# Full attention in a six-stage transformer kernel: four heads in four row strips, scores made twice, no transposed probabilities

## Chip, cores, metric

One NeuronCore of a Trainium2 chip runs the kernel alone. The metric is the device time of one execution in microseconds (us); less is better. Everything is float32 unless said otherwise.

## What is computed

Activations are 2048 tokens (4 sequences of 512) of 128 features. The reference runs six blocks on them: an expert layer, a linear attention, the expert layer again, a local-window transformer of 6 layers, a full softmax attention, and the local transformer again; each block is fed a layer norm of x and added to x. The change touches only the full attention, cut here to what matters:

```python
# 16 heads of 8 features, B=4 sequences, T=512 tokens
q, k, v, kp = heads(x @ W_Q.T), heads(x @ W_K.T), heads(x @ W_V.T), heads(x @ W_K_prime.T)
attn   = softmax(q @ k.T  / sqrt(8))      # [b, h, 512, 512]
attn_p = softmax(q @ kp.T / sqrt(8))
out = alpha * (attn @ v) + (1 - alpha) * (attn_p @ v)
x = x + merge(out) @ W_O.T
```

There are two score tables per head: one with k, one with kp. That makes 4 x 16 x 2 tables of 512x512.

## The kernel before

The kernel is one program with its instructions written out engine by engine; the engines meet at semaphores, and each engine works through its own list in the order of the code. x and its normed copy xh lie in SBUF as [feature, token] for the whole run. Between two stages all engines meet at a barrier, so a stage's time is its own. The stages are called at the end of `program`: `layernorm_block`, `expert_block` and so on; the full attention is `full_attention_block`, between the layer norms ln4 and ln5.

That stage loops over the four sequences (a hardware loop, `Fori`, on each engine). For a sequence it prepares first: TensorE projects 128 tokens at a time on `w4` (L1223, q, k, k' and v side by side). ScalarE and VectorE then split q, k and k' into three bf16 parts each (`part`, `rest`: L1294, L1297, L1362, L1365), VectorE and GpSimd lay the nine products of parts side by side in `stack` (72 rows a head, L1368, L1334), TensorE turns `stack` (L1238), and ScalarE and VectorE copy the result to `QK` (L1300, L1375). So one bf16 matmul of 72 rows makes f32-like scores.

Then come 64 units, one for each head and each 128 queries. A unit passes round the engines:

- TensorE makes both tables' scores for 128 queries x 512 keys in two PSUM banks (L1256, bf16).
- VectorE takes the negative row maximum of both banks in one operation (L1386).
- ScalarE does exp(score - maximum), with the row sum beside it (L1307, two of them, each followed by a read of the sum).
- VectorE makes the weights alpha / sum and (1 - alpha) / sum (L1391, L1393); GpSimd multiplies the first table by its weight (L1341); VectorE multiplies the second and adds (L1381, three units later).
- TensorE turns the mixed probabilities in four 128x128 blocks (L1264, four units later), and ScalarE copies them to `PT` (L1314).
- TensorE multiplies them with V (L1274, five units later) into a 32-row strip of bank 6. After 16 units ScalarE copies that bank (L1320), and TensorE multiplies with `wo_full` (L1248). At the end of a sequence VectorE adds the result to x (L1395).

The two score bank pairs (banks 0 and 1, 2 and 3) alternate from unit to unit, and so do the two turn banks (4 and 5). The steps MIX, TURN and PV (3, 4, 5 units) set how far the later steps run behind.

In the profile "psum" is any PSUM bank, and "full_x" the tile x of this stage. An f32 matmul leaves two records in the trace, a bf16 matmul and a transpose one.

Of the kernel before, what the change touches and what calls it, by code (L numbers as in the profile page):

```python
# [13 lines left out]
P = 128  # L14
# [1158 lines left out]
def full_attention_block(nc, M, W):  # L1173


    GROUP = 4 * TILES
    UNITS = AH * TILES
    MIX, TURN, PV = 3, 4, 5
    with ExitStack() as ctx:
        sem = stage_semaphores(nc, ctx, "full")  # L1180
        sb = lambda n, s, d=F32: ctx.enter_context(nc.sbuf_tensor(f"full_{n}", s, d))
        proj_full, part_ready, rest_ready, v_ready, q_stacked, k_stacked = (
            sem(n) for n in ("proj_full", "part_ready", "rest_ready", "v_ready", "q_stacked", "k_stacked"))
        stack_full, stack_act, stack_dve, prepared = (
            sem(n) for n in ("stack_full", "stack_act", "stack_dve", "prepared"))
        score_full, max_ready, exp_done, recip_ready, coef_ready, weighted, mixed = (
            sem(n) for n in ("score_full", "max_ready", "exp_done", "recip_ready", "coef_ready", "weighted", "mixed"))
        pt_full, pt_ready, out_full, out_ready, y_full, x_updated, cleared = (
            sem(n) for n in ("pt_full", "pt_ready", "out_full", "out_ready", "y_full", "x_updated", "cleared"))
        coefs = sb("coefs", [P, 2])  # L1190
        part = sb("part", [P, 2, SPLITS, 3 * D], BF16)
        rest = sb("rest", [P, 2, 2, 3 * D])
        stack = sb("stack", [P, TILES, 3, AH, STACK], BF16)
        QK = sb("QK", [STACK, 3, AH, T], BF16)
        V = sb("V", [P, TILES, AH, 32])
        negmax = sb("negmax", [P, 4, 2])
        total = sb("total", [P, 4, 2])
        recip = sb("recip", [P, 4, 2])
        weight = sb("weight", [P, 4, 2])
        prob = sb("prob", [P, 4, 2, T])  # L1200
        PT = sb("PT", [P, 2, TILES, P])
        outT = sb("outT", [P, 2, T])
        xcur = sb("xcur", [P, T])
        xcur_ready = sem("xcur_ready")
        passed, pool_passed = sem("passed"), sem("pool_passed")
        block = ctx.enter_context(nc.Block())
        B = M.bank
        QK_flat = QK[:, :, :, :].rearrange("r y h t -> r (y h t)")

        def rows(s, u):  # L1210
            return s * UNITS + u

        @block.tensor
        def _(pe):
            pe.wait_ge(M.full_loaded, 16 * M.full_dmas)
            pe.wait_ge(cleared, 3)
            with pe.Fori(0, SEQS) as s:
                for i in range(TILES):
# [339 lines left out]
```

## Time and profile before

| | us |
|---|---|
| median of 3 runs | 4995.23 |
| lowest, highest | 4987.4, 4996.35 |
| the profiled execution | 4986.6 |
| its span, first to last instruction | 4984.8 |

| engine | busy us | share of the span |
|---|---|---|
| TensorE (PE) | 4538.3 | 91% |
| TensorE weight load (PEld) | 3137.8 | 63% |
| VectorE (DVE) | 3695.8 | 74% |
| ScalarE (ACT) | 2724.3 | 55% |
| GpSimd (POOL) | 2632.8 | 53% |

These shares are an average over six blocks with different limits. The full attention runs from about 2413.6 to 3235.8 us, a sixth of the span, and only the rows of that stretch say what it waits for. Matmuls are pipelined: one record's duration takes in the drain behind its stream, and records that follow one another overlap in the trace.

### The profile page before, as it was taken

What the parts mean: (1) busy time and instruction counts of PE and PEld (TensorE: products, weight loads), DVE (VectorE), ACT (ScalarE), POOL (GpSimd) and SP (SyncE); (2) the same over time, 40 slices, a digit from 0 to 9 for tenths busy, and PEclk for the clock granted to TensorE, in tenths of its full rate; (3) what the DMA queues carried; (4) which work ended last, traced back from release to release, by engine and by line L of the source; (5) the groups of instructions that cost most, each with busy time, mean ns of one, the idle gap of its engine ahead of it and who ended that gap; (6) DMA issues with size and microseconds to landing.
All of it is one profiled execution on the core that took longest, in us unless ns stands there. A gap on an engine that the chain in (4) does not pass through costs nothing. (4 is left out here: it accounts for less than half of the span.)

```text
span 4984.8 us, 159895 instructions
## 1 busy us (share of the span) xinstructions
PE 4538.3 (91%) x69032; PEld 3137.8 (63%) x69032; DVE 3695.8 (74%) x5226; ACT 2724.3 (55%) x3635; POOL 2632.8 (53%) x3243
## 2 busy tenths in 40 slices
PE   8999979999999999999687787879999999999997
PEld 6667656666666666666454554556666666666665
DVE  3333368888888888887677686778888888888885
ACT  1111125666666666665476676736666655666663
POOL 0000036666666766665254454556666666666673
PEclk8998989999999999999798998989999999999998
DMA  1000022222222232322000000022323222222321
GB/s 53 17 0 17 17 57 63 71 74 73 70 73 68 69 77 72 76 66 56 1 1 2 2 1 1 1 78 64 78 65 77 70 74 70 73 65 66 83 65 48
DMA packets 150754, 255.76 MB, mean 51 GB/s; under 512 B 37161, under 2 KB 40753, under 8 KB 149937
## 3 DMA queue, kind: packets, MB, share of 16 engines
q1 hardware_dynamic: 150064, 245.71, 19.4%
q8 instruction: 538, 8.81, 0.7%
q14 instruction: 152, 1.24, 0.1%
HBM read 49.49 MB, written 1.05 MB: 10 GB/s over the span
## 5 line engine op out<-in xcount | busy, mean ns | idle before, releaser
L608 PE MATMUL psum<-loc_wqkv,loc_zs 128*128 128x512 f32 x2304 | 1119.3, 609 | 22.4 <-DVE loc_zs L1157 15.9
L608 PEld LDWEIGHTS psum<-loc_wqkv,loc_zs 128*128 128x128 f32 x2304 | 404.2, 192 | 375.5 <-issue 333.8
L1341 POOL TENSOR_TENSOR full_prob<-full_prob,full_weight 128x512 f32<-128x512 f32 x256 | 377.9, 1476 | 331.4 <-DVE full_weight L1393 330.9
L963 POOL TENSOR_TENSOR loc_rc_k<-loc_rc_k,loc_rs_k 128x1024 f32<-128x1024 f32 x192 | 454.9, 2369 | 141.6 <-DVE loc_rs_k L1044 141.3
L703 PEld LDWEIGHTS psum<-loc_PT,loc_V 64*64 64x64 f32 x24576 | 393.3, 135 | 196.4 <-issue 194.4
L703 PE MATMUL psum<-loc_PT,loc_V 64*64 64x32 f32 x24576 | 423.2, 220 | 47.8 <-issue 41.1
L841 ACT ACTIVATE loc_sq_k<-psum 128x1024 f32<-128x1024 f32 x192 | 196.7, 1025 | 476.9 <-PE psum L608 476.9
L963 POOL TENSOR_TENSOR loc_rc_q<-loc_rc_q,loc_rs_q 128x1024 f32<-128x1024 f32 x192 | 453.7, 2363 | 0.0
L722 PEld LDWEIGHTS psum<-loc_outT,loc_wo 128*128 128x128 f32 x3072 | 380.9, 195 | 97.8 <-issue 92.8
L1307 ACT ACTIVATE full_prob<-psum,full_negmax 128x512 f32<-128x512 f32 x512 | 347.5, 684 | 153.6 <-DVE full_negmax L1386 140.9
L938 POOL TENSOR_TENSOR loc_rt<-loc_rn 128x32 f32<-128x32 f32 x192 | 46.1, 240 | 682.2 <-DVE loc_rn L1040 682.2
L1386 DVE TENSOR_REDUCE full_negmax<-psum 128x2 f32<-128x1024 f32 x256 | 312.5, 1222 | 105.1 <-PE psum L1256 105.1
L722 PE MATMUL psum<-loc_outT,loc_wo 128*128 128x128 f32 x3072 | 381.8, 278 | 2.0 <-DVE loc_gg L1100 1.9
L969 POOL TENSOR_TENSOR loc_qk_q<-loc_rc_q,loc_rn 128x1024 f32<-128x1024 f32 x192 | 365.5, 1904 | 26.7 <-issue 0.4
L929 POOL MEMSET loc_kT<- 128x256 f32 x2 | 0.6, 312 | 710.5 <-issue 710.5
L969 POOL TENSOR_TENSOR loc_qk_k<-loc_rc_k,loc_rn 128x1024 f32<-128x1024 f32 x192 | 365.3, 1903 | 15.2
L1274 PE MATMUL psum<-full_PT,full_V 128*32 128x128 f32 x2048 | 276.3, 279 | 103.3 <-ACT full_PT L1314 88.2
L868 ACT ACTIVATE loc_PT<-psum 128x1024 f32<-128x1024 f32 x192 | 196.8, 1025 | 306.3 <-PE psum L614 306.3
L859 ACT ACTIVATE loc_outT<-psum 128x1024 f32<-128x1024 f32 x192 | 196.7, 1024 | 268.2 <-PE psum L703 268.2
L1025 DVE TENSOR_TENSOR loc_rc_k<-psum,loc_rot 128x1024 f32<-128x1024 f32 x192 | 234.6, 1222 | 137.2 <-POOL loc_qk_k L969 127.0
L677 PEld LDWEIGHTS psum<-loc_kT,loc_qT 64*32 64x32 f32 x24576 | 267.9, 105 | 105.1 <-issue 102.9
L836 ACT ACTIVATE loc_sq_q<-psum 128x1024 f32<-128x1024 f32 x192 | 197.3, 1028 | 236.2 <-PE psum L608 236.0
(170 smaller groups left out, 10131.1 us busy)
## 6 DMA issues: line engine op xcount, KB each, us to landing
loc_V<-loc_V SPq DMA_DIRECT2D x1152, 128.0 KB, 2.4
loc_V<-loc_V SPq DMA_DIRECT2D x672, 64.0 KB, 2.1
loc_wqkv<-in_wqkv SPq DMA_DIRECT2D x42, 512.0 KB, 3.7
moe_w<-in_moe_w SPq DMA_DIRECT2D x32, 256.0 KB, 3.3
loc_wo<-in_wo SPq DMA_DIRECT2D x12, 512.0 KB, 4.4
loc_w<-in_w SPq DMA_DIRECT2D x12, 341.0 KB, 3.3
loc_w<-in_w SPq DMA_DIRECT2D x12, 192.0 KB, 3.8
loc_scales<-in_scales SPq DMA_DIRECT2D x14, 128.0 KB, 3.4
```

The source lines that it names most:

```text
L608: mm = pe.matmul(M.bank[bank + g], zs[:, s, i * P:(i + 1) * P], wqkv[:, k, g * T:(g + 1) * T], start=True, stop=True)
L677: mm = pe.matmul(M.bank[YB + c][q:q + 32, p * 64:(p + 1) * 64], qT[r:r + 64, p, q:q + 32], kT[r:r + 64, p, k0:k0 + 64], start=False, stop= ...
L703: mm = pe.matmul(M.bank[WB + c][64 * j:64 * j + 64, m * P + q:m * P + q + 32], V2[r:r + 64, i, w, p * 64:(p + 1) * 64], PT[r:r + 64, p, q: ...
L722: mm = pe.matmul(M.bank[ZB][:, 0:P], wo[:, p, :], outT[:, p // (PAIRS // 2), p % (PAIRS // 2), :], start=(p == 0), stop=(p == PAIRS - 1))
L836: act.activation(sq_q[:, :], W_, ACT.Square).then_inc(q_squared, 1)
L963: pool.tensor_tensor(rc[:, :], rc[:, :], rs[:, :], ALU.add).then_inc(added, 1)
L969: pool.tensor_tensor(pair_major(out[:, :, :, :]), by_pair(rc[:, :]), spread_heads(rn[:, a:a + HEADS], DH), ALU.mult).then_inc(ready, 1)
L1025: dve.tensor_tensor(heads(rc[:, :]), heads(bank), rot[:, c, t % TILES, :].rearrange("p (o d) -> p o d", o=1).broadcast_to([P, HEADS, DH]), ...
L1274: mm = pe.matmul(B[6][32 * j:32 * j + 32, i * P:(i + 1) * P], V[:, kb, h, :], PT[:, u % 2, kb, :], start=(kb == 0), stop=(kb == TILES - 1))
L1307: last = act.activation(prob[:, n % 4, y, :], B[2 * (n % 2) + y][:, :], ACT.Exp, bias=negmax[:, n % 4, y:y + 1], accum_out=total[:, n % 4, ...
L1341: pool.tensor_tensor(prob[:, n % 4, 0, :], prob[:, n % 4, 0, :], weight[:, n % 4, 0:1].broadcast_to([P, T]), ALU.mult).then_inc(weighted, 1)
L1386: dve.tensor_reduce(negmax[:, n % 4, :], M.psum[:, 2 * (n % 2):2 * (n % 2) + 2, :], AX_X, ALU.max, negate=True).then_inc(max_ready, 1)
```

## The change

`full_attention_block` is written anew; the rest of the program is the same but for the weights' layout and two small constants.

- A **group** is four heads of one sequence; there are 16. Heads 4g to 4g+3 lie in four strips of 32 partitions, 8 features of each used, and `wqkk` holds the weights in that layout, so that one matmul projects q (or k, or k') of four heads. q, k and k' stay f32 in `qkk`; splitting, stacking and turning them is gone.
- The scores of a group are made **by query** first (L1263): a matmul of one head uses 8 rows of its strip (tile 32x128), f32, 512 keys wide. VectorE takes the negative maximum of a bank pair (L1386, two heads of one table) and writes it to `lowest`. After 16 such slots TensorE turns `lowest` (L1307, four transposes), and VectorE adds it to q (L1393) as two further rows, 8 and 9, of each strip (`shifted`). Rows 8 and 9 of k and k' are set by a bias of ones and zeros (`sel`), so a second matmul, now **by key** (L1270, 10 rows), gives score - maximum already turned: keys on the partitions, 512 queries wide.
- ScalarE takes the exponential of one such bank at a time, without a bias or a sum (L1334), into `probT`. The value matmul (L1297) takes `probT` as it is, the four heads in four column strips of one bank (tile 128x32), accumulating over four key blocks. V has a ninth column of ones, so row 8 of each strip becomes the sum.
- ScalarE copies that bank with alpha or 1 - alpha (L1354, `raw`; the sum row without), TensorE spreads the sum over its strip (L1314, an f32 matmul with `sel`), VectorE takes the reciprocal of 128x512 (L1399), and GpSimd multiplies and adds the two tables (L1362, L1364). TensorE multiplies with `wo_full` (L1319), and VectorE adds to x for each group (L1404).

The order is a plain list over steps K, the same on each engine: maxima of group u at slots 16u to 16u+15, the turn at 18, exponentials from 20 on, values from 23 on at every other step, sums at 32 and 40, output at 44. So in the steady state a slot does one maximum pair of group u and two exponential matmuls of group u-1 or u-2. Bank pairs 0-1 and 2-3 alternate between maxima, turns, sums and outputs; banks 4, 5, 6 rotate between exponentials and projections; bank 7 takes the values. Nothing loops: the code is written out.

```diff
+        def at(K, offset):
+            u, k = divmod(K - offset, SLOTS)
+            return (u, k) if 0 <= u < GROUPS else (None, None)
...
         @block.tensor
         def _(pe):
+            def take_pair(n):
+                if n >= 2:
+                    pe.wait_ge(a_free, n - 1)
+                return [B[b] for b in A_PAIRS[n % 2]]
+
+            def take_bank(n):
+                if n >= 3:
+                    pe.wait_ge(b_free, n - 2)
+                return B[B_BANKS[n % 3]]
...
+                for e in range(2):
+                    if u is not None:
+                        i, y, r = k // 4, k // 2 % 2, 2 * (k % 2) + e
+                        mm = pe.matmul(pair[e], qkk[32 * r:32 * r + AD, u % 3, 0, i * P:(i + 1) * P],
+                                       qkk[32 * r:32 * r + AD, u % 3, 1 + y, :], start=True, stop=True, skip_group_check=True)
+                        if e == 1:
+                            mm.then_inc(a_full, 1)
+                    if u2 is not None:
+                        y, kb, r = j // 8, j % 8 // 2, 2 * (1 - j % 2) + e
+                        bank = take_bank(b_nth["exp", u2, j, e])
+                        pe.matmul(bank, qkk[32 * r:32 * r + AD + 2, u2 % 3, 1 + y, kb * P:(kb + 1) * P],
+                                  shifted[32 * r:32 * r + AD + 2, u2 % 2, :], start=True, stop=True,
+                                  skip_group_check=True).then_inc(b_full, 1)
...
+                    if kb == 0 and (u or y):
+                        pe.wait_ge(values_out, 2 * u + y)
...
+                    pe.wait_ge(b_free, b_nth["exp", u, 8 * y + 2 * kb + 1, 1] + 1)
+                    for r in range(4):
+                        mm = pe.matmul(B[PV][32 * r:32 * r + 32, :], V[:, u // 4 % 2, kb, u % 4 * 4 + r, :],
+                                       probT[:, (u * 8 + y * 4 + kb) % SETS, r, :], start=(kb == 0), stop=(kb == TILES - 1),
+                                       skip_group_check=True)
+                    mm.then_inc(values_done, 1)
...
+                        bank = take_pair(a_nth[f"sum{y}", u])[0]
+                        pe.wait_ge(values_out, 2 * u + y + 1)
+                        pe.matmul(bank, M.sel[:, 0:P], raw[:, y, :], start=True, stop=True).then_inc(a_full, 1)
...
         @block.scalar
         def _(act):
...
+                        act.wait_ge(b_full, n + 1)
+                        act.activation(probT[:, (u * 8 + y * 4 + kb) % SETS, r, :], B[B_BANKS[n % 3]], ACT.Exp).then_inc(b_free, 1)
...
+                    act.activation(raw[:, y, :], B[PV], ACT.Identity, scale=coefs[:, y:y + 1]).then_inc(values_out, 1)
...
         @block.gpsimd
         def _(pool):
...
+                    pool.wait_ge(a_free, a_nth[f"sum{y}", u] + 1)
+                    pool.tensor_tensor(part[:, y, :], raw[:, y, :], part[:, y, :], ALU.mult).then_inc(scaled, 1)
+                pool.wait_ge(scaled, 2 * u + 2)
+                pool.tensor_tensor(mixed[:, :], part[:, 0, :], part[:, 1, :], ALU.add).then_inc(mixed_ready, 1)
...
         @block.vector
         def _(dve):
...
+                    dve.wait_ge(a_full, n + 1)
+                    dve.tensor_reduce(
+                        lowest[:, u % 2, i, :].rearrange("p (r e) -> p r e", e=32)[:, 2 * (k % 2):2 * (k % 2) + 2, AD + y],
+                        M.psum[:, b:b + 2, :], AX_X, ALU.max, negate=True).then_inc(a_free, 1)
...
+                    dve.tensor_tensor(shifted[:, u % 2, :], qkk[:, u % 3, 0, :], B[A_PAIRS[n % 2][0]], ALU.add).then_inc(a_free, 1)
...
+                        dve.reciprocal(part[:, y, :], B[A_PAIRS[n % 2][0]]).then_inc(a_free, 1)
...
+def sum_constant():
+
+    row, col = np.arange(P)[:, None], np.arange(P)[None, :]
+    spread = (row % 32 == AD) & (row // 32 == col // 32)
+    rows = np.stack([row[:, 0] % 32 == AD, row[:, 0] % 32 == AD + 1], 1)
+    return np.concatenate([spread, rows], 1).astype(np.float32)
```

The order on TensorE, in the unit loop of the kernel before (one round is a unit; REGISTER_ALU prepares a wait):

```order
L1254 REGISTER_ALU
L1256 MATMUL psum<-full_QK 128x512 x2
L1264 MATMUL psum<-ident,full_prob 128x128 x4
L1274 MATMUL psum<-full_PT,full_V 32x128 x4
L1254 REGISTER_ALU
L1256 MATMUL psum<-full_QK 128x512 x2
L1264 MATMUL psum<-ident,full_prob 128x128 x4
L1274 MATMUL psum<-full_PT,full_V 32x128 x4
```

And now, in steady state, the end of slot 0 of a group (the first sum), slot 1 with its values, and slot 2 with the turn:

```order
L1263 MATMUL psum<-full_qkk 128x512
L1270 MATMUL psum<-full_shifted,full_qkk 128x512
L1314 MATMUL psum<-full_raw,sel 128x512
L1263 MATMUL psum<-full_qkk 128x512
L1270 MATMUL psum<-full_shifted,full_qkk 128x512
L1263 MATMUL psum<-full_qkk 128x512
L1270 MATMUL psum<-full_shifted,full_qkk 128x512
L1297 MATMUL psum<-full_probT,full_V 32x512 x4
L1263 MATMUL psum<-full_qkk 128x512
L1270 MATMUL psum<-full_shifted,full_qkk 128x512
L1263 MATMUL psum<-full_qkk 128x512
L1270 MATMUL psum<-full_shifted,full_qkk 128x512
```

The transposes of the probabilities are gone; four score matmuls of two kinds alternate, and four value matmuls of 512 columns stand at the end of every other slot.

The order on VectorE, in the unit loop before:

```order
L1386 TENSOR_REDUCE full_negmax<-psum 128x2
L1390 REGISTER_ALU
L1391 RECIPROCAL full_recip<-full_total 128x2
L1393 TENSOR_TENSOR full_weight<-full_recip,full_coefs 128x2
L1381 SCALAR_TENSOR_TENSOR full_prob<-full_prob,full_weight 128x512
```

And now, over one group in steady state:

```order
L1399 RECIPROCAL full_part<-psum 128x512
L1386 TENSOR_REDUCE full_lowest<-psum 128x2 x2
L1393 TENSOR_TENSOR full_shifted<-full_qkk,psum 128x512
L1386 TENSOR_REDUCE full_lowest<-psum 128x2 x6
L1399 RECIPROCAL full_part<-psum 128x512
L1386 TENSOR_REDUCE full_lowest<-psum 128x2 x4
L1404 TENSOR_TENSOR x<-x,psum 128x512
L1386 TENSOR_REDUCE full_lowest<-psum 128x2 x4
```

The maxima stand alone between four rarer operations; two of them are reciprocals of 128x512 where there were 128x2.

## Rows read from the trace of the kernel before

**Rows 1.** Windows: start:end, length, busy us (instructions) by engine, granted clock, DMA.
```profile
core 0: us, PE busy (x) PEld busy (x) DVE busy (x) ACT busy (x) POOL busy (x), PEclk, DMA share, GB/s
2413.60:3235.80 822.20, 630.00 (x4416) 433.51 (x4416) 612.54 (x1163) 579.96 (x1412) 412.00 (x305) 0.93 0.00 1
2413.60:2447.50 33.90, 18.06 (x200) 14.46 (x200) 20.36 (x36) 18.94 (x29) 9.92 (x13) 0.75 0.01 2
2447.50:2619.00 171.50, 139.23 (x904) 93.59 (x904) 134.09 (x258) 126.11 (x326) 94.47 (x64) 0.96 0.00 1
2621.00:2653.00 32.00, 17.87 (x202) 14.26 (x203) 18.59 (x33) 17.63 (x28) 8.07 (x12) 0.79 0.01 2
2653.00:2826.00 173.00, 138.91 (x904) 93.42 (x902) 133.98 (x258) 127.27 (x325) 94.47 (x64) 0.96 0.00 1
```

**Rows 2.** Line L1395: durations ns min/median/max, first and last start us.
```profile
L1395 DVE TENSOR_TENSOR x<-x,psum x4: 686/686/687, 2617.9 to 3235.1; 128x512 f32 x4
```

**Rows 3.** Groups by line: busy us, mean ns of one, idle before and its releaser.
```profile
L1386 DVE TENSOR_REDUCE full_negmax<-psum 128x2 f32<-128x1024 f32 x256 | 312.5, 1222 | 105.1 <-PE psum L1256 105.1
L1381 DVE SCALAR_TENSOR_TENSOR full_prob<-full_prob,full_weight 128x512 f32<-128x512 f32 x256 | 190.8, 745 | 3.7 <-POOL full_prob L1341 3.7
L1393 DVE TENSOR_TENSOR full_weight<-full_recip,full_coefs 128x2 f32<-128x2 f32 x256 | 41.1, 160 | 8.8
L1391 DVE RECIPROCAL full_recip<-full_total 128x2 f32<-128x2 f32 x256 | 39.6, 155 | 3.9 <-ACT full_prob L1307 3.9
...
L1307 ACT ACTIVATE full_prob<-psum,full_negmax 128x512 f32<-128x512 f32 x512 | 347.5, 684 | 153.6 <-DVE full_negmax L1386 140.9
...
L1314 ACT ACTIVATE full_PT<-psum 128x512 f32<-128x512 f32 x256 | 152.1, 596 | 12.8 <-PE psum L1264 12.8
L1307 ACT ACTIVATION_READ_ACCUMULATOR full_prob<-psum,full_negmax 128x1 f32 x512 | 101.2, 198 | 0.0
...
L1341 POOL TENSOR_TENSOR full_prob<-full_prob,full_weight 128x512 f32<-128x512 f32 x256 | 377.9, 1476 | 331.4 <-DVE full_weight L1393 330.9
...
L728 PE MATMUL psum<-loc_zs,mean_w 128*128 128x512 f32 x96 | 49.1, 593 | 0.0
```

**Rows 4.** Waits from 2450 to 2618: waiter, releaser, us in total, times, longest.
```profile
POOL full_prob L1341 <- DVE full_weight L1393: 82.2, 63, 17.6
PEld psum L1274 <- ACT full_PT L1314: 36.5, 53, 1.6
ACT full_prob L1307 <- DVE full_negmax L1386: 35.2, 35, 2.2
DVE full_negmax L1386 <- PE psum L1256: 25.7, 32, 1.9
```

**Rows 5.** Timeline of TensorE in the local stage: start us, duration us, records.
```profile
1497.39 1.60 PE L677 MATMUL psum<-loc_kT,loc_qT 64*32 64x64 f32 x128
1498.92 1.98 PE L608 MATMUL psum<-loc_wqkv,loc_zs 128*128 128x512 f32 x4
...
1499.88 1.02 PE L608 MATMUL psum<-loc_wqkv,loc_zs 128*128 128x512 f32 x2
1500.83 2.46 PE L703 MATMUL psum<-loc_PT,loc_V 64*64 64x32 f32 x128
...
1504.22 1.88 PE L608 MATMUL psum<-loc_wqkv,loc_zs 128*128 128x512 f32 x4
```

**Rows 6.** Timeline of the unit loop: a copy by ScalarE and its reader.
```profile
2601.68 0.59 ACT L1314 ACTIVATE full_PT<-psum 128x512 f32<-128x512 f32 x1
2602.28 0.15 DVE L1391 RECIPROCAL full_recip<-full_total 128x2 f32<-128x2 f32 x1
2602.32 0.79 PEld L1274 LDWEIGHTS psum<-full_PT,full_V 128*32 128x32 f32 x8 [1.02 <-ACT full_PT L1314]
```

**Rows 7.** Groups by line elsewhere, for prices: a reciprocal and an exponential.
```profile
L1067 DVE RECIPROCAL loc_recip<-loc_total 128x16 f32<-128x16 f32 x192 | 48.6, 253 | 6.6
...
L864 ACT ACTIVATE loc_prob<-loc_prob 128x1024 f32<-128x1024 f32 x192 | 202.7, 1056 | 1.5
L137 ACT ACTIVATE ln_sq<-xh 128x512 f32<-128x512 f32 x24 | 15.1, 631 | 86.9 <-DVE xh L148 75.4 <-PE psum L124 11.5
```

**Rows 8.** Groups by line: the start of the stage on VectorE and GpSimd.
```profile
L1352 DVE TENSOR_SCALAR w<-w 128x128 f32<-128x128 f32 x1 | 1.7, 1744 | 0.0
...
L1328 POOL MEMSET full_V<- 128x2048 f32 x1 | 1.8, 1805 | 44.6 <-SPq L1179 44.6
```

More of the change, by code:

```diff
@@ L1206, in full_attention_block @@
+        scaled, folded = sem("scaled"), sem("folded")
+        coefs = sb("coefs", [P, 2])
+        other = sb("other", [P, 1])
+        qkk = sb("qkk", [P, 3, 3, T])
+        shifted = sb("shifted", [P, 2, T])
+        lowest = sb("lowest", [P, 2, TILES, P])
+        V = sb("V", [P, 2, TILES, AH, 32])
+        probT = sb("probT", [P, SETS, 4, T])
+        raw = sb("raw", [P, 2, T])
+        part = sb("part", [P, 2, T])
+        mixed = sb("mixed", [P, T])
         block = ctx.enter_context(nc.Block())
@@ L1207, in full_attention_block, with begins, value_step @@
         B = M.bank
-        QK_flat = QK[:, :, :, :].rearrange("r y h t -> r (y h t)")
-        def rows(s, u):
-            return s * UNITS + u
+        A_PAIRS, B_BANKS, PV = ((0, 1), (2, 3)), (4, 5, 6), 7
+        def at(K, offset):
+            u, k = divmod(K - offset, SLOTS)
+            return (u, k) if 0 <= u < GROUPS else (None, None)
+        def begins(K, offset):
+            u, k = at(K, offset)
+            return u if k == 0 else None
+        def value_step(K):
+            u, k = at(K, VALUES)
+            return (u, k // 8, k % 8 // 2) if u is not None and k % 2 == 0 else (None, None, None)
@@ new lines, in full_attention_block @@
+        a_nth, b_nth = {}, {}
+        for K in range(FIRST, LAST + 1):
+            u, k = at(K, 0)
+            if u is not None:
+                a_nth["max", u, k] = len(a_nth)
+            for name, offset in (("turn", TURN), ("sum0", SUMS), ("sum1", SUMS + 8), ("out", OUT)):
+                if begins(K, offset) is not None:
+                    a_nth[name, begins(K, offset)] = len(a_nth)
+            u, k = at(K, LATER)
+            if u is not None:
+                for e in range(2):
+                    b_nth["exp", u, k, e] = len(b_nth)
+            u = begins(K, -7)
+            if u is not None and u % 4 == 0:
+                b_nth["v", u // 4] = len(b_nth)
+            for y in range(3):
+                if begins(K, y - 6) is not None:
+                    b_nth["qkk", begins(K, y - 6), y] = len(b_nth)
@@ L1213, in _, with values_count @@
+        def values_count(u, y, kb):
+            return u * 8 + y * 4 + kb + 1
         @block.tensor
         def _(pe):
[L1215 to L1279 removed]
```

320 lines of the change are left out of this document (128 added, 192 removed).

## Prediction

> **What bounds the kernel now.** I read the windows first: one row for the whole full-attention stage, one for its preparation and one for its unit loop, of the first and the second sequence. The reader is to see that the stage takes 822.2 us of 4984.8, that the preparation takes 33.9 and 32.0 us with every engine half idle, that the loop over 64 units takes 171.5 and 173.0 us, and that no engine is full in it: TensorE 139, VectorE 134, ScalarE 126 us [rows 1]. From 2621.0 to 2653.0 and 2653.0 to 2826.0 it repeats itself; the four updates of x end the four rounds, 205.7 us apart [rows 2]. A unit is 171.5 / 64 = 2.68 us. The groups by line then say what a unit is made of [rows 3]: on VectorE 1.22 + 0.75 + 0.16 + 0.16 = 2.28 us, on ScalarE 2 x (0.68 + 0.20) + 0.60 = 2.35 us, on GpSimd 1.48. The waits say why none is full: GpSimd for the weight, the value matmuls for the copy of the transposed probabilities, the exponential for the maximum, the maximum for the scores [rows 4]. It is a ring of short handovers round engines that each have 2.3 of 2.68 us to do. So work taken off one engine alone would bring little; the change takes some off all, and what decides is what each has left and how closely the new order couples them.
>
> **What stays.** Only this stage changes: 4986.6 (the profiled execution) - 822.2 = 4164.4 us stay. The three start-up loads that become five land thousands of us before use. The stage is straight code now instead of a loop; the local stages, straight code too, hold TensorE busy, so I cost that at nothing.
>
> **Prices, each from a row.** An f32 matmul of 512 columns leaves two records. One record lasts 0.59 with its drain, and four that follow one another 1.88: (1.88 - 0.59) / 3 = 0.43 us of stream a record, 0.86 a matmul, and its result is whole at 0.43 + 0.59 = 1.02 us, as the pair of L608 shows [rows 3, 5]. The same four took 1.98 at another place: I read the 0.10 as a weight load that waited with its matmul. A change of the tile's shape costs 0.09: the last 128x512 matmul before L703 ends its stream 0.86 after its start at 1499.88, and L703 begins at 1500.83, 0.95 later [rows 5]. A handover between engines is 0.05 us: copy L1314 ends at 2602.27, its reader starts at 2602.32 [rows 6]. On ScalarE an exponential of 128x512 with bias and sum is 0.68 + 0.20. Without them it costs what a plain function does: from SBUF 1.06 for 1024 elements against 0.63 for a square of 512, the same line of 0.83 ns an element; from PSUM the copy of 512 took 0.60, and I take that [rows 3, 7]. The double-bank maximum stays at 1.22.
> The reciprocal of 128x512 has no row. Reciprocals of 2 and 16 elements take 0.155 and 0.253 us, 7.0 ns an element, hence 0.14 + 512 x 0.007 = 3.7 us [rows 3, 7]. The bounds are 0.69 (another 128x512 operation from PSUM) and, should the small ones hide part of the slope, some 4.5; I take 3.7, since it is the same operation.
> Four strips at once have no row of that size either. L677 runs 128 records of 64 columns (0.053 us each, so 6.8 in a row) in 1.60 us, over 2 row and 4 column strips: at least 4.3 at a time [rows 5]. L703, with 64-column weights, gets 3.4 us of stream into 2.46, only 1.4 at a time, but there each record streams 32 columns behind a 64-column weight load. In the new code a record streams 512 columns, so neither issue nor loads should bind: I take 0.86 us for four strips together. The other end is one by one, 3.44. Below 0.86 nothing can go.
>
> **The sum of one group of four heads (16 slots, 16 groups).** VectorE: 16 x 1.22 + 2 x 3.7 + 2 x 0.69 = 28.3 us. ScalarE: 32 x 0.60 + 5 x 0.60 + a quarter of V = 22.4. GpSimd three operations, 4.4, on nobody's path. TensorE: 16 x 0.86 for scores, 8 x (0.86 + 2 x 0.09) for values, six whole-array matmuls of 0.86 + 0.18, the turn 0.6, a quarter of V 0.2: 29.1. None of these is the time; three banks for the exponential and in-order waits make it longer.
> Take two slots, an even one and an odd one that ends with values. At 0 the even slot's four matmuls start and stream to 0.96. Its first exponential's scores are whole at 1.13, ScalarE frees the bank at 1.13 + 0.05 + 0.60 + 0.05 = 1.82. The odd slot's second exponential needs that bank (three back), so it streams from 1.82 to 1.82 + 0.10 + 0.86 = 2.79. Then the values: 0.09 + 0.86 = 3.74, and 0.09 back: **3.84 us for two slots**, 30.7 for eight pairs. The two sums and the turn stand in even slots, where TensorE would wait for the bank anyway (+0.2). Of the projections for the group ahead, the one in slot 11 is bare and finds a later exponential (+1.6); slot 12 has a projection and the output matmul (+1.0). V's share 0.3. Together 33.8.
> Now the waits on VectorE. At a reciprocal one of the two score pairs is held for 1.22 + 3.7 us: the sum's pair comes free 6.05 us after its slot began, TensorE is there at 4.0 and stands 2.1 us, with the exponentials of that slot queued behind it; twice a group. Behind the first reciprocal the turn waits for a maximum and the slot after it for another: 0.8. Values of the next table wait for the copy of `raw`, 0.3 twice. That is 5.6. **A group: 39.4 us.** VectorE would be busy 72% of it.
> The ends: preparation 16 us (two memsets of V by VectorE and one by GpSimd, of which the row of L1352 shows that they may hold each other up: 1.74 us for 128x128 beside the memset L1328 [rows 8]; four projections on a slow clock, as the 0.75 to 0.79 granted in the preparation now [rows 1]); then 20 slots with maxima alone, 1.3 each: 42 us. The last 20 slots have no maxima, 38, and the last values, copy, sum, reciprocal, three GpSimd operations, output and update follow one another, 12: 50 us. Between them are 236 slots = 14.75 groups x 39.4 = 581. **Stage: 42 + 581 + 50 = 673 us** against 822.2, and 4164.4 + 673 = 4837 us for this execution. The median of the runs shown lies 8.6 us above it, inside their spread of 9; I say 4840.
>
> **What a page adds.** By rows 5 the strips overlap 4.3-fold where eight could. The Trainium skill, "TensorE: Matmul & The Clock Gate", section on packing small matmuls, puts four row strips of 512 columns at 3.07 times one by one. The Trainium skill, "VectorE: DVE Perf Modes", section on the hardware budget of the 8-slice pipeline, has the reciprocal repeat its divide step 8 times; with that page's clock of 0.96 GHz an estimate is 4.3 us, and 0.6 more twice a group would add 18 us. The trace shows 7.0 ns an element instead of 8.3, and the sum goes by it.
>
> **Rivals.**
> Strips overlap, but not wholly (0.17). Say 1.12 us for four, a third of the way from 0.86 to the 1.6 that 4.3 of 8 would make. The bank then comes at 2.08, the pair becomes 4.35 (+0.5), a group 43.4, the stage 640 + 95 = 735: 4900. For it: no row shows more than 4.3 of 8. Against: issue alone explains those. The Trainium skill's 3.07, named above, gives this same figure.
> Half overlap (0.07): 1.6 us for four; a pair is 5.1, a group 49.5, the stage 830: no change, 5000.
> **The column strips of the values run one after another** (0.13): four moving operands, one for each strip, 128 rows high, where L677 had 64-row ones. Values take 3.44 instead of 0.86, +2.58 x 8 = 20.6 us a group, the stage 673 + 330 = 1003: 5165 us, slower. It decides from 49.5 us a group on, that is when a values step costs 1.3 us more than I say. Against: L677's eight tiles have different moving operands and reach 4.3, more than two row strips alone could. A TensorE clock that falls to 1.2 GHz in the loop would end near it; the clock was 0.96 with 81% busy [rows 1], and the new loop leaves TensorE waiting about as much, never over 3 us, so I give that part of this chance only.
> A cheap reciprocal or less coupling (0.03): without the 5.6 us of waits a group is 33.8, the stage 590: 4755.
> That the change does not do what it says (strips given but tiles of 128 rows) is in the slower rival.
>
> **How the numbers follow.** Forecast 0.60, 4840, its own range 4770 to 4885. Range for 8 in 10: from 4750 (the cheap end) to 5010 (half overlap); what is left out is the slower rival and little below. What a measurement of this kernel can tell from no change is about 0.2%, 10 us. Faster 0.60 + 0.17 + 0.03, less a little for partial overlap near half: 0.79; same 0.05; slower 0.16.
>
> **What would show it.** Steady groups 39 us apart by the updates of x; in a slot all four score matmuls starting within 0.1 us of one another and lasting about 1.0; L1297's four likewise; L1399 at 3.7 us with TensorE idle some 2 us behind each; VectorE about 70% busy. Wrong if L1263 and L1270 records start 0.43 us apart throughout (no overlap), if a reciprocal is below 2 us, or if the granted clock in the loop is far below 0.96.

## The result, and the profile after

| | before | changed |
|---|---|---|
| median | 4993.14 (4 runs) | 5105.14 (4 runs) |
| lowest, highest | 4987.4, 4996.35 | 5100.95, 5119.73 |
| the profiled execution | 4986.6 | 5119.73 |
| its span | 4984.8 | 5117.9 |

The changed kernel is slower: ratio 1.0231, 95% interval 1.0208 to 1.0254. The forecast was 4840 us with a range up to 5010; the result lies outside that range, and the change went the other way: it was to save 155 us and costs 112.

The windows of the changed kernel, columns as in [rows 1]: the whole stage (936.3 us, where it took 822.2), 480 us of the steady loop, and three neighbouring stretches inside it.

```profile
2427.90:3364.20 936.30, 907.18 (x3360) 240.60 (x3360) 439.49 (x328) 332.47 (x597) 61.12 (x49) 0.59 0.00 1
2530.00:3010.00 480.00, 473.44 (x1862) 125.09 (x1860) 239.60 (x178) 183.84 (x332) 32.91 (x26) 0.61 0.00 1
2800.00:2830.00 30.00, 29.69 (x110) 8.97 (x106) 13.93 (x11) 10.06 (x18) 2.55 (x3) 0.50 0.00 1
2830.00:2844.00 14.00, 14.00 (x80) 4.29 (x80) 7.39 (x7) 7.92 (x15) 0.58 (x1) 0.98 0.00 0
2844.00:2860.00 16.00, 15.69 (x62) 3.77 (x62) 9.01 (x7) 5.12 (x10) 1.27 (x1) 0.51 0.00 1
```

Read the busy times and the clock behind them (the last but two of the numbers) together. TensorE is busy 473 of 480 us, VectorE 240 and ScalarE 184, so TensorE now bounds the loop, and it does so with a granted clock of 0.61. In [rows 1] it was 0.93 for the stage and 0.96 in the unit loop. The 0.61 is a mixture of the two levels: 0.50 (1.2 GHz) for most of the time and 1.00 (2.4 GHz) for stretches of 7 to 17 us. The updates of x (the counterpart of [rows 2]) stand 52 to 56 us apart where 39.4 was forecast, as these two:

```profile
2786.48 0.69 DVE L1404 TENSOR_TENSOR x<-x,psum 128x512 f32<-128x512 f32 x1 [0.65 <-PE psum L1319]
2839.02 0.69 DVE L1404 TENSOR_TENSOR x<-x,psum 128x512 f32<-128x512 f32 x1 [0.65 <-PE psum L1319]
```

The groups by line, answering [rows 3]: the first two are the score matmuls, then the maximum, the exponential and the reciprocal.

```profile
L1270 PE MATMUL psum<-full_shifted,full_qkk 10*128 10x512 f32 x1024 | 499.8, 992 | 3.7 <-ACT full_probT L1334 3.7
L1263 PE MATMUL psum<-full_qkk 8*128 8x512 f32 x1024 | 439.0, 979 | 13.7 <-DVE full_lowest L1386 9.3 <-DVE full_part L1399 3.4 <-ACT full_qkk L1349 0.8
L1386 DVE TENSOR_REDUCE full_lowest<-psum 128x2 f32<-128x1024 f32 x256 | 310.6, 1218 | 396.9 <-PE psum L1263 396.8
L1334 ACT ACTIVATE full_probT<-psum 128x512 f32<-128x512 f32 x512 | 282.0, 596 | 532.7 <-PE psum L1270 532.5
...
L1399 DVE RECIPROCAL full_part<-psum 128x512 f32<-128x512 f32 x32 | 107.4, 3356 | 69.1 <-PE psum L1314 69.1
```

A score record lasts 0.98 to 0.99 us in the mean, where an f32 record of 512 columns in the stage before this one lasted 0.59 [rows 3]. VectorE and ScalarE keep their prices to the hundredth, and their idle time is all behind TensorE (396.8 and 532.5 us). TensorE hardly waits: 13.7 and 3.7 us before all its score matmuls.

The timeline of one slot and its values at the low level, then of one at the high level (start, duration):

```profile
2799.66 1.22 PE L1263 MATMUL psum<-full_qkk 8*128 8x512 f32 x1
2799.67 1.22 PE L1270 MATMUL psum<-full_shifted,full_qkk 10*128 10x512 f32 x1
...
2799.68 1.22 PE L1270 MATMUL psum<-full_shifted,full_qkk 10*128 10x512 f32 x1
2800.68 1.06 PE L1263 MATMUL psum<-full_qkk 8*128 8x512 f32 x1
...
2805.13 1.94 PE L1297 MATMUL psum<-full_probT,full_V 128*32 128x512 f32 x8
```

```profile
2742.99 0.69 PE L1263 MATMUL psum<-full_qkk 8*128 8x512 f32 x1 [0.30 <-DVE full_lowest L1386]
2743.00 0.69 PE L1270 MATMUL psum<-full_shifted,full_qkk 10*128 10x512 f32 x1
...
2743.01 0.69 PE L1270 MATMUL psum<-full_shifted,full_qkk 10*128 10x512 f32 x1
2743.52 0.59 PE L1263 MATMUL psum<-full_qkk 8*128 8x512 f32 x1
...
2744.06 1.07 PE L1297 MATMUL psum<-full_probT,full_V 128*32 128x512 f32 x8
```

So the strips do run side by side: four score matmuls start within 0.03 us of one another at either level, and the eight records of the values take 1.07 us, not 3.44. The mechanism on which the forecast stood is there. Only everything takes twice as long for most of the time: second records come 1.02 us after the first instead of 0.53, values take 1.94 instead of 1.07.

What did TensorE do before the clock rose? In the windows of 1 us it goes from 0.50 to 1.00 between 2830 and 2831, and these are the matmuls just ahead, all of them on 128 rows:

```profile
2826.45 2.08 PE L1279 MATMUL psum<-wv_full,xh 128*128 128x128 f32 x8
2828.45 1.94 PE L1297 MATMUL psum<-full_probT,full_V 128*32 128x512 f32 x8
```

All eight rises between 2540 and 2970 us come right behind such a run or within it: a projection, then values or an output. Not every run brings one: that of 2561.86 did not. Then, with mostly scores of 8 and 10 rows, the clock falls again between 2844 and 2845, although TensorE was busy for 14.00 of the 14 us ahead.

### The profile page after: what moved, and what is told of

Its sections match the earlier page's. It is cut to its first block and busy times, and to the rows that moved or that the text cites. A ratio compares the mean times of both kernels' runs of the same rounds, so it can differ in the third digit from the quotient of the medians.

```text
span 5117.9 us, 153823 instructions
## 1 busy us (share of the span) xinstructions
PE 4827.6 (94%) x67976; PEld 2954.4 (58%) x67976; DVE 3514.1 (69%) x4391; ACT 2476.0 (48%) x2820; POOL 2271.9 (44%) x2987
## 5 line engine op out<-in xcount | busy, mean ns | idle before, releaser
L1386 DVE TENSOR_REDUCE full_lowest<-psum 128x2 f32<-128x1024 f32 x256 | 310.6, 1218 | 396.9 <-PE psum L1263 396.8
L1334 ACT ACTIVATE full_probT<-psum 128x512 f32<-128x512 f32 x512 | 282.0, 596 | 532.7 <-PE psum L1270 532.5
L1270 PE MATMUL psum<-full_shifted,full_qkk 10*128 10x512 f32 x1024 | 499.8, 992 | 3.7 <-ACT full_probT L1334 3.7
L1263 PE MATMUL psum<-full_qkk 8*128 8x512 f32 x1024 | 439.0, 979 | 13.7 <-DVE full_lowest L1386 9.3
L1362 POOL TENSOR_TENSOR full_part<-full_raw,full_part 128x512 f32<-128x512 f32 x32 | 40.5, 1267 | 871.0 <-DVE full_part L1399 871.0
L677 PE MATMUL psum<-loc_kT,loc_qT 64*32 64x64 f32 x24576 | 308.4, 225 | 17.4 <-issue 17.1
```

The lines of the kernel that those rows point to most:

```text
L677: mm = pe.matmul(M.bank[YB + c][q:q + 32, p * 64:(p + 1) * 64], qT[r:r + 64, p, q:q + 32], kT[r:r + 64, p, k0:k0 + 64], start=False, stop= ...
L1263: mm = pe.matmul(pair[e], qkk[32 * r:32 * r + AD, u % 3, 0, i * P:(i + 1) * P], qkk[32 * r:32 * r + AD, u % 3, 1 + y, :], start=True, stop ...
L1270: pe.matmul(bank, qkk[32 * r:32 * r + AD + 2, u2 % 3, 1 + y, kb * P:(kb + 1) * P], shifted[32 * r:32 * r + AD + 2, u2 % 2, :], start=True, ...
L1334: act.activation(probT[:, (u * 8 + y * 4 + kb) % SETS, r, :], B[B_BANKS[n % 3]], ACT.Exp).then_inc(b_free, 1)
L1386: dve.tensor_reduce(lowest[:, u % 2, i, :].rearrange("p (r e) -> p r e", e=32)[:, 2 * (k % 2):2 * (k % 2) + 2, AD + y], M.psum[:, b:b + 2, ...
```

## The question for the experiments

Why is the granted clock 0.50 in a loop that keeps TensorE busy 99% of the time, when it was 0.96 in a loop that used it for 139 of 171.5 us [rows 1]? Three theories were set against one another.

- **A.** The score matmuls address few rows of the array: 8 or 10 of each strip of 32, where the kernel before had 72-row and 128-row operands.
- **B.** The small waits of TensorE behind VectorE, above all at the reciprocals.
- **C.** Strips as such, or the many changes between row strips, column strips and the whole array.

## Experiment 1: all 32 rows of a strip

```diff
-mm = pe.matmul(pair[e], qkk[32 * r:32 * r + AD, u % 3, 0, i * P:(i + 1) * P],
-               qkk[32 * r:32 * r + AD, u % 3, 1 + y, :], ...)
+mm = pe.matmul(pair[e], qkk[32 * r:32 * r + 32, u % 3, 0, i * P:(i + 1) * P],
+               qkk[32 * r:32 * r + 32, u % 3, 1 + y, :], ...)
...
-pe.matmul(bank, qkk[32 * r:32 * r + AD + 2, ...], shifted[32 * r:32 * r + AD + 2, u2 % 2, :], ...)
+pe.matmul(bank, qkk[32 * r:32 * r + 32, ...], shifted[32 * r:32 * r + 32, u2 % 2, :], ...)
```

> Only the height of the two kinds of score matmuls changes: all 32 rows of a strip instead of 8 (by query) and 10 (by key). The added rows are zeros in one operand or both, so the scores are the same; the number of matmuls, their columns, waits and order are the same. In the changed kernel the steady state had a granted clock of 0.60 to 0.64 with TensorE busy 98% of the stretch, four strips start within 0.03 us of one another, a slot's two records start 1.00 us apart in the slow stretches and 0.52 in the fast ones. Theory A (the clock falls because the score matmuls use few rows of the array): the granted clock of the stage rises above 0.9, a group takes 33 to 40 us instead of 54, the stage 600 to 680 us instead of 950, the program 4770 to 4860 us. Theory B (the clock falls because TensorE stands still for one or two us behind maxima, reciprocals and copies): the clock stays at 0.60 to 0.64 and the time within 1% of 5105 us. Theory C (32x128 tiles, whatever their rows, keep the clock low): as B.

Measured: 4838.03 us median (4831.21 to 4864.14, 4 runs) beside 5000.52 for the kernel before (7 runs), ratio 0.9675, interval 0.9651 to 0.97. The number of rows in the two score matmuls takes 267 us away. Its windows (the stage, the maxima alone, the same 480 us, the tail), and two updates of x:

```profile
2426.40:3112.90 686.50, 619.47 (x3360) 178.00 (x3360) 434.00 (x328) 326.03 (x597) 61.05 (x49) 0.92 0.00 1
2438.00:2480.00 42.00, 38.76 (x101) 11.65 (x96) 25.15 (x22) 3.55 (x5) 0.00 (x0) 0.56 0.00 0
2530.00:3010.00 480.00, 438.09 (x2621) 126.99 (x2620) 335.14 (x250) 252.91 (x466) 46.82 (x37) 1.00 0.00 1
3060.00:3112.00 52.00, 42.68 (x108) 8.65 (x104) 10.31 (x4) 13.20 (x24) 6.31 (x5) 0.50 0.00 0
```

```profile
2727.26 0.69 DVE L1404 TENSOR_TENSOR x<-x,psum 128x512 f32<-128x512 f32 x1 [0.65 <-PE psum L1319]
2765.70 0.69 DVE L1404 TENSOR_TENSOR x<-x,psum 128x512 f32<-128x512 f32 x1 [0.65 <-PE psum L1319]
```

The clock is 1.00 throughout the loop with TensorE busy *less* (438 of 480 instead of 473) and with the same changes of shape. A group takes 38.4 us. A stands, B is hard to hold, since TensorE waits more than before, and C falls: the strips and the changes are all still there.

## Experiment 2: no reciprocals

```diff
-dve.reciprocal(part[:, y, :], B[A_PAIRS[n % 2][0]]).then_inc(a_free, 1)
+dve.tensor_copy(part[:, y, :], B[A_PAIRS[n % 2][0]]).then_inc(a_free, 1)
```

> The two reciprocals of 128x512 per group (3.36 us each) become copies of the same shape (about 0.69 us), so this leaves the division out; the rows of the score matmuls stay 8 and 10. Theory A (few rows): the waits behind the reciprocals go, the granted clock stays at 0.60 to 0.64, a group takes 50 to 53 us instead of 54, the program 5060 to 5100. Theory B (standing still): with the longest stands gone the clock rises to 0.8 or more, a group falls below 45 us, the program below 4950.

Measured on the changed kernel (8 and 10 rows; the division by the sums is left out): 5138.78 us in one run. The 480 us of the loop:

```profile
2530.00:3010.00 480.00, 476.44 (x1826) 125.95 (x1822) 192.35 (x174) 179.95 (x324) 32.98 (x26) 0.59 0.00 1
```

VectorE has 47 us less to do (192 instead of 240), and the clock is no higher and the time no shorter. B falls. But the time is also longer than theory A had it (5060 to 5100 us): twelve groups take 662 us instead of 645, and why is not shown.

## Experiments 3 and 12: stretches of one kind

These two kernels leave out the reference's computation. They run stretches of f32 matmuls of 512 columns on TensorE with nothing to wait for.

```diff
+def strips(pe, rows, n):
+    for j in range(n):
+        for r in range(4):
+            pe.matmul(B[r], x[32 * r:32 * r + rows, (j % 4) * P:(j % 4 + 1) * P],
+                      x[32 * r:32 * r + rows, T:2 * T], start=True, stop=True, ...)
```

> This kernel leaves all six blocks out and stores x as it was loaded. It runs ten stretches of f32 matmuls of 512 columns on TensorE, each without any wait, 12 us of rest before each: (1) four row strips of 8 rows, 120 matmuls; (2) 16 rows; (3) 24 rows; (4) 32 rows; (5) one strip of 32 rows alone, 40; (6) the whole array, 40; (7) the whole array with data in 8 rows and zeros in the others, 40; (8) four column strips of 128x32, 120; (9) eight matmuls in strips of 8 rows, then four in column strips, ten times, as the slots of the changed kernel; (10) the same with 32 rows. Theory A (few rows): granted clock 0.5 in 1, rising with the rows towards 1.0 in 4; 6 and 8 at 0.9 or more, 9 at 0.5 to 0.7, 10 at 0.9 or more. Theory B (standing still): there is none here, so all stretches reach 0.9 or more. Theory C (row-strip tiles): 1 to 5 all 0.5. Four strips of 32 rows should stream a round of four in 0.86 us plus a weight load at full clock, four column strips in 0.86; if one of them goes one by one it takes 3.4.

Timeline of the first: four strips of 8, 16, 24, 32 rows; one strip of 32; the whole array; the whole array with data in 8 rows and zeros in the others (`small`); four column strips.

```profile
27.66 51.58 PE L1418 MATMUL psum<-x 8*128 8x512 f32 x240 [27.66 <-PEq L1475]
87.41 51.58 PE L1418 MATMUL psum<-x 16*128 16x512 f32 x240 [8.17 <-PEq L1475]
147.16 29.17 PE L1418 MATMUL psum<-x 24*128 24x512 f32 x240 [8.17 <-PEq L1475]
184.51 27.57 PE L1418 MATMUL psum<-x 32*128 32x512 f32 x240 [8.18 <-PEq L1475]
220.27 68.60 PE L1438 MATMUL psum<-x 32*128 32x512 f32 x80 [8.18 <-PEq L1475]
297.02 36.20 PE L1442 MATMUL psum<-x 128*128 128x512 f32 x80 [8.16 <-PEq L1475]
341.38 36.21 PE L1446 MATMUL psum<-small 128*128 128x512 f32 x80 [8.15 <-PEq L1475]
385.74 27.58 PE L1424 MATMUL psum<-x 128*32 128x512 f32 x240 [8.15 <-PEq L1475]
```

Sixty rounds of four records (an f32 matmul is two records) take 51.58 us with 8 or 16 rows (0.86 a round) and 27.57 with 32 (0.46), and two stretches of the whole array take the same whether its data are dense or zero in 120 of 128 rows. So it is the rows that the instruction addresses, not what stands in them.

Its last two stretches go much as the slots of the changed kernel, with nothing to wait for: eight matmuls in row strips (16 records), then four in column strips (8 records), ten times over; first with 8 rows in the row strips, then with 32. From each, one repeat:

```profile
427.09 3.80 PE L1418 MATMUL psum<-x 8*128 8x512 f32 x16
430.82 1.94 PE L1424 MATMUL psum<-x 128*32 128x512 f32 x8
...
494.27 2.00 PE L1418 MATMUL psum<-x 32*128 32x512 f32 x16
496.20 1.06 PE L1424 MATMUL psum<-x 128*32 128x512 f32 x8
```

A repeat takes 5.60 us in all ten with 8 rows, at 0.50, and 2.93 us with 32 rows once the clock has risen, at 1.00. The changes of shape are the same, and there are no waits: B and C fall here a second time.

One thing was unclean: the windows print 1.00 for everything before 180 us, the first two stretches too. A rival could say that 8 and 16 rows are served two strips at a time at full clock. Hence a second such kernel, in another order:

> It leaves out the reference's computation: eleven stretches of f32 matmuls of 512 columns on TensorE alone, 240 records each (whole array: 80, the last: 480), with a pause between them. In e3_stretches the trace has no clock record for the first two stretches (8 and 16 rows), and their level stood only on their durations. Here they come after stretches that raise the clock: whole array, four strips of 32 rows, of 8, of 32, of 16, of 32, of 20, of 24 rows, two strips of 32 rows one beside the other, whole array, four strips of 8 rows again. Theory (what counts is how many of the array's rows the matmuls address): strips of 32 and 24 rows about 28 us each at a granted clock near 1.00; strips of 8 and 16 rows fall to 0.50 and take 51 us; two strips of 32 rows address as many rows as four of 16 and fall too, 2 x 60 rounds at 0.86, 103 us; the whole array 36 us at 1.00; 20 rows decides where between. Rival (8 and 16 rows are served two strips at a time at full clock, and the 1.00 printed for them was true): 51 us with a granted clock of 1.00, and two strips of 32 rows about 55 us at 1.00.

Its windows of TensorE: four strips of 8 rows, of 32, of 16, of 20, of 24, then two strips of 32. Behind them the timeline of the stretches of 8 rows, of 24, and of two strips.

```profile
109.00:160.00 51.00, 50.84 (x240) 0.50 0.00 1
169.00:196.00 27.00, 27.00 (x236) 0.93 0.00 1
205.00:256.00 51.00, 51.00 (x240) 0.50 0.00 1
...
301.00:352.00 51.00, 51.00 (x240) 0.50 0.00 1
361.00:389.00 28.00, 28.00 (x236) 0.89 0.00 1
398.00:500.00 102.00, 102.00 (x240) 0.50 0.00 0
```

```profile
109.16 51.58 PE L1418 MATMUL psum<-x 8*128 8x512 f32 x240 [8.18 <-PEq L1487]
...
360.37 29.39 PE L1418 MATMUL psum<-x 24*128 24x512 f32 x240 [8.17 <-PEq L1487]
397.93 102.77 PE L1470 MATMUL psum<-x 32*128 32x512 f32 x240 [8.18 <-PEq L1487]
```

The levels repeat, and the windows now show a level for each. Every stretch shown begins at 0.50: behind the stretch of 32 rows that ends at 101 us the clock falls in the pause, between 104 and 105, before the 8 rows begin. Four strips of 24 or 32 rows then rise to 1.00 (the 32 rows that start at 168.91 between 172 and 173, hence 0.93 over their window; the 24 rows at about 367). Four strips of 8, 16 or 20 rows never rise, in 51 us. Two strips of 32 rows stay at 0.50, 102.77 us for 120 pairs (0.86 a pair). TensorE is busy all the time in every one of these stretches.

## Experiments 5, 9 and 6: half of the matmuls, and 16 rows

The first gives 32 rows to the scores by key alone, the second to the scores by query alone (one half each of the diff of experiment 1), the third puts 16 for both.

> The changed kernel with 32 rows for the scores by key alone (L1270); the scores by query (L1263) keep 8 rows. Half of the score matmuls then address the strip wholly. Theory 1 (what counts is the share of rows that TensorE's matmuls address over time): the granted clock of the loop comes out between that of the changed kernel (0.60) and that of e1_rows32 (1.00), and a group between 54 and 38.5 us. Theory 2 (any matmul with few rows keeps the clock at half): clock near 0.60, 5100 us. Theory 3 (half of them is enough): clock 0.95 or more, about 4840 us.

> The other half of e5_by_key_rows32: 32 rows for the scores by query (L1263) alone, 10 rows for those by key (L1270). There are as many matmuls of the one kind as of the other. If what counts is the share of rows addressed and not which matmul addresses them, this comes out like e5: granted clock 0.80 to 0.90 in the loop, about 4925 us (4890 to 4970). If the matmuls by key decide (their exponentials are the longer queue), it stays near the changed kernel, 5050 to 5110 us. In the head, where the scores by query stand alone, two strips of 32 rows are in use at a time, and e1_rows32 shows 0.56 there: the same is expected here by both.

> The changed kernel with 16 rows of each strip in both score matmuls instead of 8 and 10. In e3_stretches four strips of 16 rows stayed at half clock, 24 and 32 rows did not. If that carries over, the granted clock of the loop stays near 0.60 to 0.65, groups 50 to 54 us apart, and the program takes 5050 to 5110 us. If instead the clock follows the rows in proportion, 16 rows lie a third of the way from 8 to 32, and the program comes near 5010 us.

Measured, one run each, beside a kernel before of 5003.27 (e5, e6) and 5000.38 (e9): 4926.84, 4906.05 and 5044.46 us, in the order of the texts above. The same 480 us of the loop, in that order:

```profile
2530.00:3010.00 480.00, 445.23 (x2410) 126.25 (x2407) 309.04 (x230) 234.44 (x430) 44.22 (x35) 0.90 0.00 1
```
```profile
2530.00:3010.00 480.00, 439.85 (x2558) 124.81 (x2554) 327.27 (x243) 245.60 (x452) 45.88 (x37) 0.97 0.00 1
```
```profile
2530.00:3010.00 480.00, 457.75 (x2072) 123.68 (x2073) 265.83 (x197) 201.09 (x365) 37.90 (x30) 0.73 0.00 1
```

It is neither matmul by itself: either half brings most of the gain, 178 and 199 of the 267 us. The clock is 0.90 and 0.97, between 0.61 and 1.00; e9 was expected at 0.80 to 0.90 and came out above. In e5 the updates of x stand 38.4 us apart in most groups and 50 to 52 in every third or fourth: groups at the high level, broken by a stretch at the low one. In e9 they stand 38.4 and 40.0 apart in turn, so its groups take 39.2 us in the mean and those of e5 41.8; the difference repeats within each trace, though there is one run of each. The halves aren't quite alike: the score matmuls address 20 rows in the mean in e5 (8 and 32) and 21 in e9 (32 and 10). In that order, 9, 16, 20, 21 and 32 rows, the loop's clock is 0.61, 0.73, 0.90, 0.97 and 1.00; whether the mean decides or the order of the matmuls, no run separates. With 16 rows the loop is at 0.73: higher than with 8 and 10 rows and higher than the 0.60 to 0.65 expected, with 5044 us just below the range given, and still slower than the kernel before. A stretch of nothing but such matmuls stays at 0.50 (e12); the loop also has matmuls of 128 rows, and the rises read above stand behind them.

## Experiment 4: what the waits on VectorE cost

Experiment 1 with copies in place of the reciprocals (the division is left out).

> Both score matmuls take all 32 rows of a strip, as in e1_rows32, and a copy stands in place of each 128x512 reciprocal; it leaves out the division by the sums. This prices the waits on VectorE, which were invisible at half clock. Theory of the prediction: the waits behind the reciprocals cost 2 x 2.1 us and 0.8 at the turn in each group, so with 0.7 us in place of 3.35 a group goes from 38.5 to 33.5 to 34.5 us, 14.75 groups bring 60 to 74 us, and the program takes about 4765 to 4780 us against 4838. Rival (the waits are small, because the queue of exponentials covers most of them): a group stays above 37 us and the program above 4810. The granted clock of the loop stays 0.95 or higher by both.

Measured: 4813.09 us in one run. Two updates of x:

```profile
2674.73 0.69 DVE L1404 TENSOR_TENSOR x<-x,psum 128x512 f32<-128x512 f32 x1 [0.65 <-PE psum L1319]
2711.86 0.69 DVE L1404 TENSOR_TENSOR x<-x,psum 128x512 f32<-128x512 f32 x1 [0.65 <-PE psum L1319]
```

Groups of 36.0, 36.0, 36.0 and 37.1 us repeat: 36.3 in the mean against 38.4. So the long reciprocals cost 2.1 us a group more than copies would, not the 5.0 that the prediction had for them (twice 2.1, and 0.8 at the turn). The result lies between what the two theories gave, nearer to the rival.

## Experiments 8, 10 and 11: the division in four pieces

Experiment 1, and VectorE copies the sum bank to SBUF, which frees the bank, and divides in four pieces of 128 columns, one behind each of the next maxima; `raw` has two buffers and the output comes three slots later.

```diff
-dve.reciprocal(part[:, y, :], B[A_PAIRS[n % 2][0]]).then_inc(a_free, 1)
+dve.tensor_copy(spread[:, y, :], B[A_PAIRS[n % 2][0]]).then_inc(a_free, 1)
...
+dve.reciprocal(part[:, y, c * w:(c + 1) * w], spread[:, y, c * w:(c + 1) * w]).then_inc(divided, 1)
```

> As e1_rows32 (32 rows of each strip), and the reciprocal no longer reads PSUM: VectorE copies the sum bank to SBUF (0.7 us), frees the bank, and divides in four pieces of 128 columns, one after each of the next four maxima; the output is three slots later, the copied values have two buffers. VectorE's work grows by 1.4 + 6 x 0.1 us a group. Theory of the prediction: a bank pair is then held for 0.7 us instead of 3.35, most of the 5.6 us of waits a group go, a piece of 0.9 us per slot fits beside a maximum of 1.22, and a group takes about 35.5 us: 4838 - 14.75 x 3 = about 4795 us, ratio to the kernel before 0.959. Rival (the loop hangs on the order of the slots and not on the long operation, or the pieces delay each maximum by 0.9 us and the pairs come late four times instead of once): a group of 38 us or more, 4830 to 4870 us.

> e1_rows32 once more, beside e11_pieces_again on the same chip, since the two lie only half a per cent apart and came from different calls: 4838 us, ratio 0.9675 expected.

> e8_rows32_pieces once more: 4812 us, ratio 0.963. By the distance of the updates of x (35.2 us against 38.5) it should be 15 x 3.3 = 49 us below e10_rows32_again; by the medians of the two earlier calls 26 us. If the first holds, something outside the stage was 20 us dearer in one of the calls; if the second, the stage gives something back.

| | median us | ratio to before, interval |
|---|---|---|
| e1_rows32 | 4838.03 (4 runs) | 0.9675 (0.9651 to 0.97) |
| e10_rows32_again | 4853.58 (5 runs) | 0.9712 (0.9693 to 0.9732) |
| e8_rows32_pieces | 4812.42 (4 runs) | 0.9631 (0.9599 to 0.9663) |
| e11_pieces_again | 4830.98 (5 runs) | 0.9662 (0.9644 to 0.9681) |

e10 and e11 ran on one chip: 22.6 us apart. In e8 the updates of x stand 36.5 us apart, and VectorE is busy 371 of 480 us:

```profile
2750.37 0.69 DVE L1416 TENSOR_TENSOR x<-x,psum 128x512 f32<-128x512 f32 x1 [1.53 <-PE psum L1322]
2786.83 0.69 DVE L1416 TENSOR_TENSOR x<-x,psum 128x512 f32<-128x512 f32 x1 [1.53 <-PE psum L1322]
```
```profile
L1411 DVE RECIPROCAL full_part<-full_spread x128: 893/943/954, 2497.7 to 3052.3; 128x128 f32<-128x128 f32 x128
```

The steady groups are 36.5, and each fourth 37.5, in the mean 36.75, 1.65 less than in e1; twelve such groups are 20 us, close to the 22.6 between the medians. A group of 36.75 lies between the 35.5 of the one theory and the 38 or more of the other. The two kernels took 16 and 19 us longer than in their earlier runs. The 49 us that I expected in the text of e11 took in the ends of the stage, where the clock differs from execution to execution: the last two updates are 32.9 and 20.0 us behind the ones ahead of them in e8, 47.1 and 26.9 in e11. Both versions are faster than the kernel before, and their medians lie some 250 to 290 us below the changed kernel's.

## Why the prediction was wrong

**The failed step is the clock.** Every duration of TensorE in the sum was taken at 2.4 GHz (granted clock 1.00); the loop ran at 0.61, and a group took 54 us instead of 39.4. The prediction gave a fall to 1.2 GHz one sentence, inside the rival of 0.13, and argued from TensorE's busy share and the length of its waits. The traces show that this was the wrong thing to look at: 99% busy at 0.61 in the changed kernel, 91% at 1.00 in experiment 1. The rows of this stage in the kernel before showed no such case: its matmuls had 72 or 128 rows, at 0.93. The change's own line, eight rows of a strip of 32, was the warning, and it had no price in any row. What an unseen kind of operation does to the clock should have been a rival of its own. A granted clock far below 0.96 did stand among the signs of being wrong, and it was the one that came true.

**That this step carries the miss** is shown by experiment 1: with 32 rows the program takes 4838 us, 267 less, where the forecast of 4840 was 265 too low. That the two agree to 2 us is partly luck: the same kernel took 4854 us another time, and in the profiled execution (4864) the group is 1.0 us below the forecast, which is worth 15 us, while the ends lie 28 and the other stages 14 above it. The rival that gave nearly the right number (5165, column strips one by one) had the wrong mechanism: L1297's eight records take 1.07 us at full clock.

Step by step, from experiment 1, where the clock is as assumed:

- **Strips together, 0.86 us a slot.** Nearly right: 0.97 from a slot's start to the next in the free slots, because the second record comes 0.53 behind the first and not 0.43. The pair of slots is 3.94 us against 3.84. By e3 four strips of 32 rows take 0.46 us a round where a record of the whole array takes 36.20 / 80 = 0.45, almost fourfold. The Trainium skill, "TensorE: Matmul & The Clock Gate", section on packing small matmuls, gives 3.07 for this; the trace doesn't agree: e3 shows 3.9, and in the loop 3.44 / 0.97 makes 3.5. The rival of partial overlap (1.12 us for four, a pair of 4.35 us, 4900) stands further from the 0.97 and the 3.94 than the forecast does.
- **A group, 39.4 us.** Measured 38.4, but by two errors that partly cancel. Without the reciprocals it is 36.3 (experiment 4) where the prediction's terms make 33.8 + 0.6 = 34.4: eight pairs are 31.5 instead of 30.7, and the sums, the turn, the projections, the output and the copy of `raw` 4.8 instead of 3.7. The waits on the reciprocals are 2.1 and not 5.0. I read this as VectorE, 70% busy (335 of 480), catching up in the next slots; which slots give it back wasn't measured apart.
- **The reciprocal, 3.7 us.** 3.35. From the pieces, (3.348 - 0.943) / 384 is 6.3 ns an element (an estimate: the one reads PSUM, the other SBUF), against 7.0 from the small ones. The estimate of 4.3 from the Trainium skill, "VectorE: DVE Perf Modes", section on the hardware budget of the 8-slice pipeline, was further off.
- **Handover 0.05, exponential 0.60, maximum 1.22, values 1.04 with both changes of shape.** 0.60 and 1.22 hold; the values take 1.00 from their start to that of the next slot. The handover wasn't read again.
- **The ends, 92 us.** 686.5 - 14.75 x 38.4 = 120 us. For most of the 28 us more I read the clock again: in the slots with maxima alone only two strips work at a time, and so do they in the last slots, with scores by key alone; the windows show 0.56 in the one and 0.50 in the other, even with 32 rows. With maxima alone a slot takes 2.0 us (22 maxima from 2438.9 to 2481.2) where the prediction had 1.3, and TensorE is busy 39 of 42 us. Two strips of 32 rows stay at 0.50 in experiment 12 too. The last update comes 38.0 us behind the one ahead of it in experiment 1, and 20.0 in e8, where the clock happened to hold (0.93 from 3005 to 3059).
- **What stays, 4164.4 us.** 5119.73 - 936.3 = 4183 in the changed kernel's profiled execution, 4864.14 - 686.5 = 4178 and 4811.0 - 642.1 = 4169 in those of experiments 1 and 8. The other stages move by 10 to 20 us from run to run, and the execution profiled before was a quick one: its kernel's medians beside the experiments are 5000 to 5003.

## What to carry to other kernels

When heads are packed into strips of TensorE's rows, let the matmul address the whole strip, with zeros in the rows that aren't used: it cost nothing here (27.57 us against 51.58 for the same columns) and it made the difference between 2.3% slower and 3% faster. For every stage read the granted clock beside the busy share; a TensorE that is 99% busy at a clock of 0.61 isn't at its limit. And when a change brings a kind of operation of which the trace has no row, ask what it does to the clock, besides what it costs.

## What the runs showed of the hardware

- In stretches of nothing else, four row strips of 8, 16 or 20 rows ran at 1.2 GHz although TensorE was never idle, four of 24 or 32 rows at 2.4 GHz; one or two strips of 32 rows ran at 1.2 GHz (e3, e12). The whole array ran at 2.4 GHz even with zeros in 120 rows (80 records in 36.21 us, against 68.60 for one strip).
- In e12 the clock fell from 1.00 to 0.50 in a pause of TensorE (between 104 and 105 us; the stretch had ended at 101); in the changed kernel it also fell with TensorE busy 14.00 of 14 us.
- Four column strips of 32 columns with four different moving operands run together: 240 records of 512 columns in 27.58 us.
- In e3 the windows print 1.00 up to 180 us, for stretches whose rounds take 0.86 us as at 0.50; durations tell the level there.
- A reciprocal of 128x512 from PSUM takes 3.35 us, of 128x128 from SBUF 0.94.
- Left open: the reason for the low level with few rows, what decides in a mixture of matmuls, and the ends of the stage, which still run at 0.50 to 0.60; a version that fills them wasn't run.
